# A four-layer model on one core: routing in pairs of tiles, and attention's first loads from ACT's queue

## What is computed

```python
x = _layernorm(x + _L0_attn_ref(x, ...))   # a selective state-space scan (mamba), 2 sequences of 2048
x = _layernorm(x + _L0_ffn_ref(x, ...))    # a tree-gated feed-forward layer
x = _layernorm(x + _L1_attn_ref(x, ...))   # causal attention, 16 query heads, 4 key heads, rotary positions
x = _layernorm(x + _L1_ffn_ref(x, ...))    # mixture of 64 experts, the best 8 for each token
```

```python
q = (hidden_states @ Wq).reshape(b, s, H, D).transpose(0, 2, 1, 3)
k = (hidden_states @ Wk).reshape(b, s, HKV, D).transpose(0, 2, 1, 3)
v = (hidden_states @ Wv).reshape(b, s, HKV, D).transpose(0, 2, 1, 3)
...
logits = x.astype(jnp.float32) @ gate_w.astype(jnp.float32).T
scores = jax.nn.softmax(logits, axis=-1)
topk_w, topk_ids = jax.lax.top_k(scores, TOP_K)
topk_w = topk_w / (topk_w.sum(axis=-1, keepdims=True) + 1e-20)
```

## Time and profile before

| | |
|---|---|
| median of 3 runs | 4956.44 us (4953.86 to 4956.68) |
| the profiled execution | 4955.58 us |
| its span, first to last instruction | 4953.8 us |
| mean granted PE clock | 0.946 of full speed |
| busy share: PE, DVE, ACT, GpSimd | 87%, 70%, 56%, 38% |
| mean rate of DMA | 77 GB/s |

### The profile page before, as it was taken

The page is one execution under the profiler, slowest core; times in us unless marked ns, Lnnn a source line. Parts: engine busy times, 40 slices in busy tenths (PEclk is TensorE's granted clock), DMA queues, the critical chain, the costliest instruction groups (busy, mean ns, idle before and its releaser), DMA issues. The chain is left out here.

```text
span 4953.8 us, 82016 instructions
## 1 busy us (share of the span) xinstructions
PE 4293.2 (87%) x19960; PEld 3014.1 (61%) x19991; DVE 3476.8 (70%) x7241; ACT 2793.3 (56%) x6564; POOL 1868.3 (38%) x1544
## 2 busy tenths in 40 slices
PE   7888888699999979999999999999966559999970
PEld 3333333256665468888888888888755437777750
DVE  7999999943444878888888888888744443333348
ACT  7777777422221068888888888888733224444430
POOL 5998998600000031212122121212145543333347
PEclk8999999999999999999999999999977779999985
DMA  1000000021102531211212121212154335545558
GB/s 43 13 13 13 13 27 9 13 82 60 44 17 97 178 85 26 52 35 51 52 26 52 30 55 26 52 26 55 43 168 140 132 111 155 156 151 156 157 170 300
DMA packets 307111, 382.04 MB, mean 77 GB/s; under 512 B 123328, under 2 KB 237248, under 8 KB 300880
## 3 DMA queue, kind: packets, MB, share of 16 engines
q1 hardware_dynamic: 233936, 262.09, 17.7%
q0 software_dynamic: 26112, 73.44, 4.1%
q10 hardware_dynamic: 46944, 45.16, 3.3%
HBM read 227.78 MB, written 152.76 MB: 77 GB/s over the span
## 5 line engine op out<-in xcount | busy, mean ns | idle before, releaser
L1739 DVE TENSOR_TENSOR probsT<-ps_t,probsT 128x512 fp32r<-128x512 f32 (+3 forms) x1280 | 779.8, 609 | 136.3 <-ACT probsT L1679 115.7
L1679 ACT ACTIVATE probsT<-ps_t 128x512 fp32r<-128x512 f32 (+3 forms) x1280 | 685.4, 535 | 257.4 <-PE ps_t L1527 234.0
L1671 ACT ACTIVATE probs<-ps_s,negm 128x512 f32<-128x512 f32 (+3 forms) x1297 | 811.3, 626 | 27.7 <-DVE negm L1732 26.6
L1539 PE MATMUL ps_o<-probsT,vbuf 128*128 128x512 f32 (+3 forms) x2560 | 815.6, 402 | 6.9 <-ACT folding L1685 6.2
L1514 PE MATMUL ps_s<-kbuf,qbuf 128*128 (+1 forms) x2602 | 766.5, 379 | 58.7 <-ACT probs L1671 32.4
L1719 DVE TENSOR_REDUCE pmax<-ps_s 128x1 f32<-128x512 f32 (+3 forms) x1301 | 778.2, 601 | 46.9 <-PE ps_s L1514 22.9
L1527 PE MATMUL ps_t<-idn,probs 128*128 128x128 f32 x4352 | 695.2, 275 | 13.9 <-DVE probsT L1739 13.9
L527 POOL TENSOR_TENSOR dBx<-u,b_all 128x1024 f32<-128x1024 f32 x255 | 611.8, 2410 | 96.3 <-DVE h L623 66.6
L1527 PEld LDWEIGHTS ps_t<-idn,probs 128*128 128x128 f32 x4352 | 517.6, 142 | 134.6 <-DVE probsT L1739 41.0
L1622 POOL CAST qbuf<-room_a 128x512 fp32r<-128x512 f32 x132 | 82.8, 627 | 1264.0 <-DMA room_a<-q_scr 772.1
L1514 PEld LDWEIGHTS ps_s<-kbuf,qbuf 128*128 128x128 f32 x2602 | 444.1, 189 | 178.1 <-issue 63.9
(11 more groups left out here) (272 smaller groups left out, 6966.4 us busy)
## 6 DMA issues: line engine op xcount, KB each, us to landing
room_b<-xs ACTq DMA_DIRECT2D x294, 136.0 KB
room_c<-y SPq DMA_DIRECT2D x36, 1024.0 KB, 4.9
room_a<-q_scr SPq DMA_DIRECT2D x528, 64.0 KB
room_a<-W_guT SPq DMA_DIRECT2D x64, 384.0 KB
q_scr<-rot SPq DMA_DIRECT2D x64, 256.0 KB, 2.9
attn<-ostage SPq DMA_DIRECT2D x128, 128.0 KB
at<-attn SPq DMA_DIRECT2D x32, 512.0 KB
room_a<-W_downT SPq DMA_DIRECT2D x64, 192.0 KB
```

The lines of the kernel that those rows point to most:

```text
L1539: last = nc.tensor.matmul(ps_o[:, lo:], vbuf[:, kb, :, :], probsT[:, g % SLOTS, part, lo:], start=kb == 0 and part == 0, stop=kb == BAND * ...
L1671: nc.scalar.activation(probs[:, k, at:at + n, :], ps_s[:, u % RING, 0:n * P], ACT.Exp, bias=negm[:, tile, :], accum_out=sums[:, s, j, c:c ...
L1679: nc.scalar.activation(probsT[:, g % SLOTS, 0, lo:], ps_t[:, t % 2, lo:], ACT.Copy).then_inc(high_t.sem, 1)
L1739: nc.vector.tensor_tensor(probsT[:, g % SLOTS, 1, lo:], ps_t[:, t % 2, lo:], probsT[:, g % SLOTS, 0, lo:].bitcast(F32), ALU.subtract).then ...
```

## The change

**`qkv`.** `attention_first_loads` leaves SyncE's stream. ACT's loop over chunks is cut in two halves of 4 chunks. Between them ACT waits until SyncE's stores of the first half have landed, and issues the same 21 loads from its own queue.

**`route`.** Everything goes by pairs p of tiles (16 rounds). PE's `places(p)` is 5 small matmuls, `turn_x(p)` and `logits(p)` serve both tiles. The small per-token steps of DVE and ACT are one instruction for both tiles where the operation takes two columns. The softmax division goes: the best 8 are chosen from the exponentials themselves, and the weights are divided by their sum plus 1e-20 of the whole sum (`denom`, `share`). `r3` and `x3` have four slots. GpSimd waits once per pair and issues 16 DMAs. The overflow turn is at tile 28 (`TURN`). DVE's stream puts the refinement steps among the picks, and the sums r among the choosing.

```diff
@@ qkv, SyncE
-            attention_first_loads(sp, attn_front, q_scr, k_scr, v_scr)
@@ qkv, ACT
+            with act.Fori(0, CHUNKS // 4) as i:
+                take_v(i)
+            for o in qk_out:
+                act.wait_ge(o.sem, o.at(CHUNKS // 2 - 1))
+            for o in v_out:
+                act.wait_ge(o.sem, o.at(CHUNKS // 4 - 1))
+            attention_first_loads(act, attn_front, q_scr, k_scr, v_scr)
+            with act.Fori(CHUNKS // 4, CHUNKS // 2) as i:
+                take_v(i)
@@ route, PE
+            for p in range(-1, PAIRS):
+                if p >= 0:
+                    places(p)
+                if p + 1 < PAIRS:
+                    turn_x(p + 1)
+                if p + 2 < PAIRS:
+                    turn_attn(2 * p + 4)
+                if p + 1 < PAIRS:
+                    logits(p + 1)
+                if p + 2 < PAIRS:
+                    out_proj(2 * p + 4)
+                    turn_attn(2 * p + 5)
+                    out_proj(2 * p + 5)
@@ route, ACT
+            for p in range(-1, PAIRS):
+                if p + 1 < PAIRS:
+                    take_x(p + 1)
+                if p + 2 < PAIRS:
+                    take_attn(2 * p + 4)
+                if p + 1 < PAIRS:
+                    exps(p + 1)
+                    spread(2 * p + 2)
+                if p + 2 < PAIRS:
+                    take_attn(2 * p + 5)
+                if p + 1 < PAIRS:
+                    spread(2 * p + 3)
+                if p + 2 < PAIRS:
+                    inv_std(p + 2)
@@ route, GpSimd
-            for t in range(NT):
-                pool.wait_ge(copied.sem, copied.at(t))
-                pool.wait_ge(dest_ready.sem, dest_ready.at(t))
+            for p in range(PAIRS):
+                pool.wait_ge(copied.sem, copied.at(2 * p + 1))
+                pool.wait_ge(dest_ready.sem, dest_ready.at(p))
                 pool.sem_inc(seen.sem)
-                s = t % SLOTS
-                for k in range(TOPK):
+                for s in (2 * p % SLOTS, 2 * p % SLOTS + 1):
+                    for k in range(TOPK):
@@ route, DVE
-                nc.vector.reciprocal(erec[:, :], esum[:, :]).then_inc(step.sem, 1)
-                after(t, 1)
-                nc.vector.tensor_scalar(sc[:, :], ex[:, :], erec[:, :], None, ALU.mult).then_inc(step.sem, 1)
+                for h in range(2):
+                    last = nc.vector.max(top[:, h, :], ex[:, h, :])
+                last.then_inc(step.sem, 1)
...
+                nc.vector.scalar_tensor_tensor(denom[:, :], esum[:, :], 1e-20, tsum[:, :], ALU.mult, ALU.add).then_inc(step.sem, 1)
...
+                nc.vector.reciprocal(share[:, :, 0], denom[:, :]).then_inc(step.sem, 1)
```

More of the change, by code:

```diff
@@ L2043, in out_proj, with turn_x @@
                 last.then_inc(op_ps.sem, 1)
[L2045 to L2050, removed]
-                last.then_inc(tx.sem, 1)
[L2053 to L2058, removed]
+            def turn_x(p):
+                for h in range(2):
+                    pe.wait_ge(x3_ready.sem, x3_ready.at(2 * p + h))
+                    if p and not h:
+                        pe.wait_ge(xT_ev.sem, xT_ev.at(p - 1))
+                    for k in range(KD):
+                        last = nc.tensor.transpose(ps_x[:, KD * h + k, :], x3[:, (2 * p + h) % SLOTS, k * P:(k + 1) * P], idn[:, :])
+                last.then_inc(tx.sem, 1)
@@ L2059, in logits @@
+            def logits(p):
+                pe.wait_ge(xT_ev.sem, xT_ev.at(p))
+                if p:
+                    pe.wait_ge(ex_done.sem, ex_done.at(2 * p - 1))
+                for h in range(2):
+                    for k in range(KD):
+                        last = nc.tensor.matmul(ps_g[:, h, 0:EXPERTS], xT[:, h, k, :], w_g[:, k, :], start=k == 0, stop=k == KD - 1)
                 last.then_inc(lg.sem, 1)
             def overflow():
-                pe.wait_ge(counted.sem, counted.at(T0 - 1))
@@ L2255, in choose @@
-                nc.vector.tensor_scalar(rank_of[:, s, :], rank_of[:, prev, :], float(P * TOPK), None, ALU.add)
-                after(t, 8)
-                nc.vector.tensor_scalar(xe[:, s, :, DM + 1], top[:, :], tsum[:, :], None, ALU.mult).then_inc(step.sem, 1)
+                for h in range(2):
+                    last = nc.vector.match_replace(rest[:, h, :], top[:, h, :], ex[:, h, :], -1.0)
+                last.then_inc(step.sem, 1)
+                for h in range(2):
+                    last = nc.vector.max_index(idx[:, h, :], top[:, h, :], ex[:, h, :])
@@ new lines, in open_send, with picks @@
+            def open_send(p):
+                if p == LATE:
+                    overflow()
+                dve.wait_ge(step.sem, step.at(p))
+                dve.wait_ge(pos_ps.sem, pos_ps.at(p))
+                nc.vector.tensor_tensor(both[:, :], chosen[:, p % 2, 0, :], chosen[:, p % 2, 1, :], ALU.add).then_inc(summed4.sem, 1)
+                if p >= LATE:
+                    spilled(p)
+            def picks(p, first, end):
+                ranks = pos if p >= LATE else ranks_of(p)
+                for n in range(first, end):
+                    h, k = divmod(n, TOPK)
+                    last = nc.vector.scalar_tensor_tensor(junk[:, h, k, :], iota_sb[:, :], idx_f[:, h, k:k + 1], ranks[:, h, :],
+                                                          ALU.is_equal, ALU.mult, accum_out=dest_f[:, h, k:k + 1])
+                if end == 2 * TOPK:
+                    last.then_inc(picked.sem, 1)
@@ new lines, in close_send @@
+            def close_send(p):
+                s = 2 * p % SLOTS
+                dve.wait_ge(picked.sem, picked.at(p))
+                nc.vector.tensor_copy(dest[:, s:s + 2, :], dest_f[:, :, :]).then_inc(dest_ready.sem, 1)
+                dve.wait_ge(summed4.sem, summed4.at(p))
+                nc.vector.tensor_tensor(macc[:, :], macc[:, :], both[:, :], ALU.add).then_inc(counted.sem, 1)
+            for t in range(2):
+                add_sums(t)
+            for t in range(2):
+                add_stats(t)
```

375 lines of the change are left out of this document (196 added, 179 removed).

## The result

The changed kernel took 5011.24 us (median of 3 runs, 5008.86 to 5011.29) against 4956.44: ratio 1.0108, interval 1.0093 to 1.0122, slower by 55 us. Forecast: 5006.

| from, to | before | after | difference |
|---|---|---|---|
| start to the last copy of v in the projections | 1729.03 | 1726.73 | -2.3 |
| last copy of v to attention's first copy | 15.10 | 8.38 | -6.7 |
| to routing's first load | 1834.0 | 1836.0 | +2.0 |
| to the first burst of GpSimd | 33.9 | 40.4 | +6.5 |
| first to last burst, 15 pitches | 400.75 | 452.15 | +51.4 |

A forecast was written before the change was run, and what follows sets the result against it. Routing was taken as bound by GpSimd's 20.2 us of scatter DMAs a pair plus 6.7 us waiting for targets, with signals arriving late. Sum: 4955.6 - 8 (loads) + 49 (pitch) + 9 (start) = 5006 us, range 4890 to 5090.

The forecast's parts named there:

- The loads, -8: Projections into attention: moving 21 loads to ACT's queue saves 8 us; 2.5 us of waiting for v's last store stay.
- Fewer DVE steps, 0: Routing: fewer and wider DVE steps are worth nothing by themselves, since DVE is busy 12 of 27 us.
- The cycle, 17.2 to 22 us: Routing's new loop over pairs: 17.2 us at PE's higher clock, about 22 at 1.2 GHz.
- The pitch, 30: Routing, burst to burst: 30 us a pair with out_proj(2p+5)'s signal held too; +49 us over 15 pitches.
- rival B: Routing: signals held to the end of GpSimd's transfers, turn_attn's too; 33 to 36 us a pair, 5052 to 5097; chance 0.11.
- Case A: Routing: signals held to the end of GpSimd's transfers; 28.6 to 31.5 us a pair, 4984 to 5029; likeliest, chance 0.44.
- signals are held until 3 us after GpSimd's last DMA has ended: Routing: PE's signals, if held so, put the last of them 24 us after dest.
- Rival C, a price per signal: Routing: delay is a price per signal, not a hold to the end; faster, 4886 to 4931, most likely 4920; chance 0.31.
- The start, +9: Routing's first burst needs two tiles' targets: 7.5 us for the second tile and 1.6 for 8 more picks, +9.
- The overflow turn, taken at 0: Routing: the overflow turn one tile earlier is two small matmuls, costing 0.

The follow-up runs named there:

- both turns early: Changed kernel with two buffers aT, both turns and copies ahead of logits: 4994.23 us, ratio 1.0080 on the holding chip; 4860.44 and 4859.77 us on the others.
- the last run: Changed kernel with two buffers aT, both turns and copies ahead of logits, no hold, on the chip that holds signals: 4994.23 us, ratio 1.0080.

## Why the prediction was right, and where it wasn't

- *The loads, -8:* -6.7 in the trace, -5.7 alone on another chip. Mechanism right, term too large. ACT issued at 0.50 each, as taken. What was undersized is the tail that stays: from SyncE's last issue to attention's start 5.2 us instead of the 1.4 of before, so 3.8 are left of the wait for v's store and the unused input tile, not 2.5.
- *Fewer DVE steps, 0:* DVE's busy time in a pair fell from 12 to 8.4 us, and the pitch rose. As forecast. On the chips without holds GpSimd alone sets the pitch, 20.3 us with either kernel, so there too the saved DVE time was worth nothing.
- *The cycle, 17.2 to 22 us:* 19.8 and 18.4 in the trace without holds, with out_proj at 3.72 to 4.50 us. Right, and under GpSimd's 20.3. But 5.4 us is not out_proj at 1.2 GHz: the granted clock over the 5.41 of rows 4 was 0.68, so both levels stood in it. At 0.56 out_proj took 6.56 us (the eighth burst above), so the 22 was too low for the lower level throughout.
- *The pitch, 30:* 30.1 over the 15 pitches, but the two parts of the sum were both wrong, and that they cancelled is luck. I let the hold last to 24 us and 6.5 us stand behind it, with out_proj(2p+5)'s signal as the last held. In 10 of the 15 pitches the trace shows turn_attn(2p+5)'s as the one that counts, in the pair shown released at 18.5 with 12.6 behind. That is the chain of rival B, with an earlier release. B's 36 us needed the hold to run to the end; forced to do so, it gave 34.3. Case A is there in three pairs (the first, seventh and eighth, 29.1 to 29.8 us), and it is the bound that both turns early ran into (29.0). The step that failed is "signals are held until 3 us after GpSimd's last DMA has ended", taken for all of them: it fits a signal that is still awaited when the burst ends (22.6 in the last run, 23 before), and not the turn's, posted at 7.5 and released at 17 to 18.5.
- *Rival C, a price per signal:* it forecast 22 to 25 us a pair for fewer signals, and the pitch rose to 30.1.
- *The start, +9:* +6.5. The overflow turn, taken at 0, showed one pitch of 33.1, 3 above the mean, and the last pitch was 22.1 where it was 24.2; the two nearly cancel.
- *What I had not considered:* that the held signals may be there or not for one and the same program. The 1.1% is the change's loss where they are; where they are not it is 0.07%, not told from none. I speak of chips because time and chip always went together: the kernel before took 4856 to 4862 us in 40 executions on two chips and 4948 to 4960 in 8 on the third. But each chip was used in one stretch of time, so something else at work in that hour is not excluded.

What holds the signals remains open: I saw it only from about 7 us into GpSimd's bursts to 3 us behind them, on one of three chips and in the first pair of traces, for signals of PE and DVE and for PE's own issue. That GpSimd's transfers under way are needed rests on its absence before the first burst and after the last; that its waiting is, was only argued. SyncE's loads and stores run in the same stretch, and no kernel took them away. One clue stands in every trace with holds: in the eighth and fourteenth burst GpSimd's second DMA starts 2.83 us after its first instead of 1.26, and in just these two signals come early (ACT's second copy at 11.4 and 8.1 us in the changed kernel, r at 19.2 and 18.5 in the kernel before). No run tested what this means.

A kernel better than both is the first experiment: the routing of before with the loads on ACT's queue, 5.7 us under the kernel before where it ran (11 runs). On the chip that holds it was not run.

## What to carry to other kernels

Read what stands behind the last signal of a loop, and when it is posted, before you merge rounds: pairing saved 3.6 us of DVE's time a pair, put a turn's copy and a projection behind one late signal, and two tiles' picks instead of one's behind the last. A load for the next stage belongs on an idle queue in the middle of this one, if its data is ready there. And where a profile shows waits that the program's own releasers don't explain, run the kernel on another chip before designing for them.

## What the hardware showed that I had not expected

- The same program took 4956 us on one chip and 4860 on two others, all of it in one stage: pitch 26.9 against 20.3 us.
- In a held stretch signals came out one behind the other, and the last about 3 us behind the burst. In the first pair of the changed kernel shown above, signals posted 6.7, 7.1 and 7.5 us into a burst of 16 indirect DMAs came at 12.1, 14.3 and 18.5 us; in the last run one posted at 12.4 came at 22.6.
- PE stood still for up to 1.39 us between two matmuls with no wait between them, in the held stretch alone.
- 16 indirect DMAs of 128 rows ran at 1.26 us each on all three chips, held signals or not.
